# Token scatters freed from the score loop's pace and the first expert block spread over more quarters, in a four-layer kernel

## The reference, cut to what matters

```python
# layer 2's experts (layer 3: 16 experts, top 2, hidden 256, with biases)
topk_w, topk_idx = jax.lax.top_k(softmax(x @ router_w), 4)        # 32 experts
topk_w = topk_w / topk_w.sum()
act = silu(x @ w_gate[e]) * (x @ w_up[e]);  eo = act @ w_down[e]  # hidden 96
routed = sum over the 4 chosen e of topk_w * eo
sh = (silu(x @ sh_gate) * (x @ sh_up)) @ sh_down * sigmoid(x @ sh_gate_w)
```

## Time and profile before

| | |
|---|---|
| median of 3 runs | 1893.88 us (1890.02 to 1895.83) |
| the profiled execution | 1893.88 us, span 1892.1 us |
| busy | PE 1400.0 us (74%), DVE 1310.7 (69%), ACT 956.5 (51%), POOL 298.7 (16%) |
| mean granted TensorE clock | 0.806 |

### The profile page before, as it was taken

One profiled execution on the slowest core, in us unless ns is written; L12 is line 12 of the kernel. 1 busy time (PEld: TensorE's weight loads), 2 busy tenths in 40 slices (PEclk: granted clock), 3 DMA queues, 4 the chain that ended last, 5 costly groups with the idle time before them and its releaser, 6 DMA issues.

```text
span 1892.1 us, 22512 instructions
## 1 busy us (share of the span) xinstructions
PE 1400.0 (74%) x6401; PEld 624.9 (33%) x6402; DVE 1310.7 (69%) x4037; ACT 956.5 (51%) x2225; POOL 298.7 (16%) x388
## 2 busy tenths in 40 slices
PE   6888889874144420357888899798898899999984
PEld 2444544442011110121245555222332334434431
DVE  5988979897898886568566656677676555555552
ACT  2988888972444444103445555444444444444452
POOL 0201011020000000015550010544105200000014
PEclk7989999898555555555699999778786899999995
DMA  3010102001400000021513223222203601111112
GB/s 112 16 65 1 68 1 72 1 1 62 155 1 1 1 1 1 17 85 35 165 41 102 83 78 97 81 53 64 38 30 93 158 25 28 25 56 46 43 29 57
DMA packets 151441, 98.44 MB, mean 52 GB/s; under 512 B 73328, under 2 KB 136117, under 8 KB 151265
## 3 DMA queue, kind: packets, MB, share of 16 engines
q1 hardware_dynamic: 143543, 84.01, 15.0%
q0 software_dynamic: 6144, 12.60, 2.4%
q10 hardware_dynamic: 1632, 0.39, 0.1%
HBM read 60.83 MB, written 35.73 MB: 51 GB/s over the span
## 4 chain that ended last, share of the span: by engine, by line
PE 47%; DVE 33%; issue 9%; ACT 6%; DMA 2%; another core or an unknown queue 1%; SPq 1%; DVEq 0%; ACTq 0%
PE PS L483 39%; DVE RA L1593 5%; PE PS L479 5%; DVE nmx L1346 4%; DVE RA L1595 4%; DVE RA L1150 4%; DVE RA L1153 3%; PE PS L831 2%; DVE RB L1153 1%; DVE RB L1150 1%; DMA RA<-xd 1%; DVE RA L1309 1%; PE PS L820 1%; DVE RA L1311 1%
## 5 line engine op out<-in xcount | busy, mean ns | idle before, releaser
L483 PE MATMUL PS<-RA 72*128 72x512 bf16 (+2 forms) x1360 | 467.3, 434 | 97.0 <-DVE nmx L1346 50.2
L1346 DVE TENSOR_REDUCE nmx<-PS 128x1 f32<-128x512 f32 x512 | 348.0, 685 | 206.2 <-PE PS L483 169.2
L1791 ACT ACTIVATE RA<-PS 128x512 f32<-128x512 f32 x512 | 302.1, 598 | 293.7 <-PE PS L483 238.0
L483 PEld LDWEIGHTS PS<-RA 72*128 72x128 bf16 (+3 forms) x1360 | 120.7, 104 | 411.7 <-issue 207.1
L483 PE MATMUL PS<-RA,Vs 128*32 128x512 f32 x1240 | 225.8, 727 | 0.7 <-ACT RA L1791 0.7
L1919 ACT ACTIVATE RA<-RA 128x8 f32<-128x8 f32 x511 | 107.5, 210 | 168.0 <-DVE RA L1593 167.2
L479 PE MATMUL PS<-ident,RB 128*128 128x128 f32 (+1 forms) x329 | 62.0, 333 | 137.3 <-DVE RB L1525 123.3
L1971 POOL DMA_INDIRECT RA<-yd,RA x96 | 93.3, 972 | 417.9 <-DMA yd<-RA 270.1
L483 PE MATMUL PS<-RB,RA 128*128 (+2 forms) x672 | 151.0, 342 | 4.6 <-DVE RA L1326 4.6
L483 PE MATMUL PS<-RB 128*128 (+3 forms) x280 | 106.8, 517 | 45.0 <-ACT RB L1893 28.7
L1737 ACT ACTIVATE RA<-RA,nm 128x512 f32<-128x512 f32 x192 | 128.8, 724 | 5.2 <-POOL nm L2034 5.1
(11 more groups left out here) (299 smaller groups left out, 2032.9 us busy)
## 6 DMA issues: line engine op xcount, KB each, us to landing
RA<-scr SPq DMA_DIRECT2D x288, 96.0 KB
xd<-Otok SPq DMA_DIRECT2D x36, 256.0 KB, 3.2
RA<-xd SPq DMA_DIRECT2D x72, 128.0 KB, 2.3
scr<-parts SPq DMA_DIRECT2D x48, 128.0 KB
yd<-RB SPq DMA_DIRECT2D x48, 128.0 KB, 1.9
RB<-in_L_ffn_W SPq DMA_DIRECT2D x24, 256.0 KB
scr<-parts SPq DMA_DIRECT2D x64, 48.0 KB
yd<-RA SPq DMA_DIRECT2D x48, 64.0 KB, 1.5
```

What stands on the lines that cost most here:

```text
L483: return e.matmul(o, l, r, start=first, stop=last)
L1346: e.tensor_reduce(nmx[:, (g + lx) % 3, c:c + 1], bank[(6, 0)[i % 2]], AX.X, ALU.max, negate=True).then_inc(*ROWMAX.up(layer, n, i))
L1791: e.activation(chunk(layer, k, i), bank[(1, 5)[i % 2]], ACT.Exp).then_inc(*EXP.up(layer, k, i))
```

## The change

Three edits in the schedule; no arithmetic changes.

```diff
-    plan = {2: spread(expert_steps(0), 17, 2.3), 3: spread(expert_steps(1), 27, 2.25)}
+    plan = {2: spread(expert_steps(0), 14, 2.05), 3: spread(expert_steps(1), 27, 2.25)}
...
-    LOGITS, ..., RANK_DONE, SCATTER_FROM, LOAD_FROM = (0, 2), 3, 4, 18, 24, 26, 30, 45
+    LOGITS, ..., RANK_DONE, SCATTER_FROM, LOAD_FROM = (0, 2), 3, 4, 18, 24, 26, 37, 45
...
         def step(layer, n, i):          # POOL
             at_ = 4 * n + i - ROUTE_LATE[layer] - SCATTER_FROM
-            if 0 <= at_ < 16 * topk[layer - 2]:
-                pool.wait_ge(ROWMAX, layer, n, i)
-                scatter(layer - 2, at_)
+            if at_ >= 0:
+                for s_ in range(3 * at_ // 2, 3 * (at_ + 1) // 2):
+                    if s_ < 16 * topk[layer - 2]:
+                        scatter(layer - 2, s_)
             for task in plan[layer][0].get((n, i), ()):
                 expert_step(layer - 2, task)
```

More of the change, by code:

```diff
@@ L395, in spread @@
         return slots, [t for s in steps[at:] for t in s]
-    plan = {2: spread(expert_steps(0), 17, 2.3), 3: spread(expert_steps(1), 27, 2.25)}
+    plan = {2: spread(expert_steps(0), 14, 2.05), 3: spread(expert_steps(1), 27, 2.25)}
     assert not plan[2][1]
-    LOGITS, ROUTE_FROM, GATE_AT, EXP_AT, RANK_AT, RANK_DONE, SCATTER_FROM, LOAD_FROM = (0, 2), 3, 4, 18, 24, 26, 30, 45
+    LOGITS, ROUTE_FROM, GATE_AT, EXP_AT, RANK_AT, RANK_DONE, SCATTER_FROM, LOAD_FROM = (0, 2), 3, 4, 18, 24, 26, 37, 45
     ROUTE_LATE = {2: 0, 3: READY3[3] + 8 - 4 * LEAD}
```

## The result

| | before | after |
|---|---|---|
| median, four runs each | 1893.81 us (1890.02 to 1895.83) | 1955.53 us (1948.68 to 1962.01) |
| ratio, 95% interval | | 1.0327 [1.0289, 1.0367] |
| the profiled execution | 1893.88 us, span 1892.1 | 1963.65 us, span 1961.8, clock 0.797 |

What follows compares the result with a forecast made beforehand. No one engine was taken to bound throughout: DVE in quarters 0 to 55, PE in 68 to 175. Terms -2.3 - 3.5 - 1 + 0 + 0 - 3.1 + 5 = -4.9 us gave 1889 us, range 1879 to 1901.

Steps and rivals of the forecast that it cites:

- Part 2: Scatters without the row-maximum wait: 64 issued 1.27 us apart, ending near 948 us, no wait added; 0 of its own.
- Part 1: Experts dealt out from quarter 56 at lower density: terms of -2.3, -3.5 and -1 us, 0 behind quarter 184.
- I take -1 us ... at worst 0: Quarters 96 to 175: lower list density leaves PE less idle, -1 us; bounds -7.4 and 0.
- -3.5 us: Quarters 68 to 95: PE's idle time falls from 9.75 to 6.2 us; bounds 0 and -6.2 us.
- The clock term: Quarters 56 to 67: items raise PE's clock earlier, half the half-clock loss goes, -2.3 us; bounds -4.6 and +12.
- Part 3: POOL's bias passes move to 843.8 us: -3.1 us at the old place, +5 us beside DVE's adds, +2 net.
- blocked out: Rival: DVE's chained adds each wait for a POOL pass, 9.9 us instead of 5; 1894 us, chance 0.12.
- The combine stretch: Behind quarter 184: the same 64 combines spread over more quarters; 0, with 4 us to either side.
- The clock stays down: Rival: PE stalls on its first items and clock holds 0.50 until quarter 68; +9, 1903 us, chance 0.08.
- Density pays: Rival: from quarter 68 PE idles as little as in layer 3; sum -14, 1880 us, chance 0.2.

Runs made afterwards that it cites:

- e5: The changed kernel measured again on another chip; 1854.7 us, ratio 1.0051 to the kernel before.
- e16: The kernel before with only the scatters' row-maximum wait removed; one run, 1914.13 us against 1876.81 us for the kernel before.
- e18: The changed kernel with the scatters' row-maximum wait put back; one run, 1921.45 us against 1881.11 us for the kernel before.
- e15: The changed kernel measured once more; one run, 1963.26 us against 1876.81 us for the kernel before.
- e2: The changed kernel with the row-maximum wait put back and the old expert list; 1841.73 us, ratio 1.0004 to the kernel before.
- e1: The changed kernel with the row-maximum wait put back ahead of each scatter; 1854.63 us, ratio 1.0063 to the kernel before.
- e9: The changed kernel with SP's expert entries issued ahead of the stack loads in quarters 84 to 183; 1846.93 us, ratio 1.0007 to the kernel before.
- e4: The kernel before with only the scatters' row-maximum wait removed; 1839.12 us, ratio 0.9964 to the kernel before.
- e10: The kernel before with SP's expert entries issued ahead of the stack loads in quarters 96 to 183; 1843.43 us, ratio 1.0029.

## Why the prediction was wrong

Forecast 1889 us in a range of 1879 to 1901; measured 1955.53. On quiet chips the same change costs 0.5% (e5), some 8 us, where I had 5 us of gain: there the size is wrong; in the first comparison a mechanism was missing.

**Part 2 failed, and with it the prediction: "Free, 64 scatters 1.27 us apart ... No wait is added ... 0".** The interval was right: POOL issued them 1.27 us apart. The addresses came at 875.97 us and the last scatter at 958.90, where I had 866.6 and 948 us (5.9 us of this is the late quarter 0). But I looked only for who waits behind the scatters in POOL's order, not for what 83 us of unbroken indirect DMAs do to the others. The row-maximum wait that the change removes was a throttle: POOL could not run on while DVE stood still. e16 against its kernel before (one line, +37 us, quarters 44 to 55 at 56.9 us) and e18 against e15 (the same line put back: 26.3 instead of 74.6 us) show it, each in single runs, the second pair on two chips. A state that worsened between two runs would explain either pair alone; against it, the three prone traces without the wait have 56.9 to 74.6 us in these quarters, and the two with it 22.6 and 26.3. That the stall feeds itself without the throttle is my reading; no run shows it by itself. What the trace of before had to offer was there: DVE's and ACT's waits for a releaser without a name, 58 us over the whole span with both engines added (38 us where waits at the same time count once), 27 of them at POOL's scatters and the rest at its gathers. I passed over them as noise; of all this has only the 1% of the chain. What makes a run prone to it, and what is late, the product or its signal, stays open.

**Part 1, from quarter 96: "I take -1 us ... at worst 0", with -3.5 us before it.** The clock term came in: quarters 56 to 67 took 22 us at a clock of 0.96 to 1.00, where I expected 28 to 30 (24 entries cost less than the 12 us that I gave them; from e2 to e1 they add 8.1 us, 20.9 against 12.8). Quarters 80 to 95 went from 36.5 to 31.9 us, better than the 34 I named. But the sum of quarters 56 to 183 grew: 276.3 to 281.1 us in the first comparison, 267.8 to 281.6 us from e2 to e1. I priced the density of the list and not its phase. A list that starts three steps earlier and runs at another rate puts its `rows` entries into other quarters, and the one of quarter 112 met SP's six stack loads just when PE was near. I named "without a wait of L820 for `xd`" for quarters 80 to 95 only, where after has none; it came in quarter 116: 4.1 us in one wait in after and 4.4 us in e1. The clock was at 0.50 for 38 us of quarters 56 to 183 in both, against 25 us in before and 17 us in e2. e9 took this meeting away and about 8 us with it. Part 1 as a whole was forecast at -6.8 us and measured at +4.8 us, mis-sized by 12 us, and "at worst 0" was no bound.

**Part 3 was right in its mechanism, and 2 us too dear.** The passes moved to 849.66 us and took 8.0 us instead of 9.9. POOL's timeline of after, against the earlier trace rows:

```profile
847.57 2.14 POOL L1957 TENSOR_TENSOR parts<-QK,parts 128x1024 bf16<-128x1024 f32 x1
849.66 2.10 POOL L1985 CAST RA<-RB 54x2304 bf16<-54x2304 f32 x1
...
857.24 0.45 POOL L2003 TENSOR_TENSOR RB<-RB 18x128 bf16<-18x128 f32 x1
...
875.97 1.21 POOL L1980 DMA_INDIRECT xd<-XN,RA  x1 [18.28 <-DVE RA L1252]
```

DVE's groups beside them and in their old place, against the earlier trace rows:

```profile
L1211 DVE TENSOR_TENSOR RB<-RB 128x32 bf16<-128x32 bf16 x16 | 5.0, 312 | 0.4
...
L1283 DVE TENSOR_TENSOR RB<-RB 128x512 f32<-128x512 f32 x4 | 2.8, 692 | 0.1
L1286 DVE TENSOR_TENSOR RB<-RB 128x512 f32<-128x512 f32 x4 | 2.7, 682 | 0.0
L1278 DVE TENSOR_TENSOR RB<-RB,rs 128x512 f32<-128x512 f32 x1 | 0.7, 692 | 0.0
```

The six products are back at 0.69 us (-3.1 us in quarters 36 to 39, 12.6 to 9.5), and quarters 0 to 23 take 42.3 instead of 38.2 us: +4.1 where I had +5, and 1.4 us more come back in quarters 24 to 35, so the net is nothing instead of +2. The adds were not blocked out: 16 of them took 5.0 us instead of 2.7, less than the 9.9 of that rival. The first of the adds took 0.99 us and ended at 853.77 us, with the POOL pass beside it (853.73). The Trainium skill's rule on the shared ports ("SBUF — State Buffer", Who interferes with whom) agrees with these two sets of rows.

**The combine stretch** moved by less than 4 us, as said: 137.5 against 139.7 us. Inside it more moved than the 4.8 us that I had each way, 9.2 us less in quarters 184 to 255 and 7.0 us more in 256 to 271, where 15 combines stand instead of 8; from e2 to e1 it was 4.8 us less and 4.9 us more. Layer 3 in the first comparison lost 4.6 us in quarters 344 to 367, where its own free scatters are issued; e15 shows 9.3 us there and one such wait of 12.4 us. I had counted 0.

**The rivals.** "The clock stays down" did not happen where I put it, in quarters 56 to 67, but its mechanism (PE waits for an input, and the clock falls and doubles what follows) is what the list cost later. "Density pays" never came: the old list idles no more than the new one. None of them held the stall.

## What to carry to other kernels

A wait that looks useless may be what keeps an engine in step with the others: before it goes, ask not only who is queued behind it but how long its engine then runs unbroken, and look in the trace for waits without a named releaser beside the same instructions. When a list of steps is dealt out anew, look at its phase and not only its density: the load that an engine needs next must not stand behind a burst of loads on the same queue (e9 against e5). And a gain seen once is worth a second measurement on another chip or day: the line that gave 0.4% in e4 cost 2% in e16.

## What the runs showed of the hardware

- While POOL issues indirect DMAs (128 rows each) 1.27 us apart, DVE and ACT can wait up to 24.5 us for a matmul of PE that the record gives 0.61 us. This was in all five traces from measurements where the kernel before took 1877 to 1894 us (DVE's and ACT's waits added, over the whole span: 58 us in 16 waits in before, 141 us in 26 in after, 121 us in 17 in e15, 100 us in 16 in e16 and 105 us in 21 in e18), and in none of the other 15 traces, which issue the same indirect DMAs at the same pace. The longest came beside SP's weight loads as well; 9.27 us in before came without them.
- The same kernel took 1838 us in one measurement and 1894 us in another, 3% apart. No quiet trace of the kernel before is on record; e10, which differs from it in SP's order alone, has a span 52.7 us shorter than the prone one, 15.4 us of that in quarters 344 to 367 beside layer 3's scatters, 7.4 us in quarters 44 to 55 and 6.9 us in 56 to 67.
- In e5 a wait of PE of 4.12 us ended at 1042.02, and the clock was at 0.50 for 10.2 us from 1042.3 us. Quarters 112 to 127 took 8.6 us more than in e9, which has no such wait and no half clock there: about half of it the wait, the rest the same 182 matmul records running longer.
- A load of 128-row tiles that SP issued right behind six stack loads took 7.6 us to land in e1 and 6.4 us in e2, where the median was 2.2 us.
